# Leaving out the matmuls that TensorE runs beside the triangular solve, in an attention and expert layer on one core

## The reference, cut to what matters

```
h = silu(causal_conv4(rms(x)))
q, k, v = norm(h @ wq), norm(h @ wk), h @ wv
mem = 0.9 * mem + (h @ w_spike)_t                 # membrane
spike = mem > 0.5;  mem = mem - 0.5 * spike
alpha = sigmoid(ab_t + alpha_spike * spike);  beta = sigmoid(bb_t + sum(spike * beta_spike))
s = s * alpha
s = s - beta * k (k' s) + beta * k v'             # delta rule, s is 64 x 128 for each head
out = q' s
```

## Time and profile before

| | |
|---|---|
| median of 3 runs | 2338.61 us (2329.96 to 2342.53) |
| span of the profiled execution | 2335.2 us; its own time outside the span is not given |
| TensorE busy | 1920.2 us (82%), 18624 records |
| VectorE busy | 1336.8 us (57%) |
| ScalarE, GpSimd busy | 692.3 us (30%), 287.5 us (12%) |
| mean granted TensorE clock | 0.895 |
| the matmuls of L836 | 230.8 us busy, 480 records |

### The profile page before, as it was taken

How to read it: one execution, slowest core, us unless ns; L and a number is a source line. 1 busy time by engine, 2 the same in 40 slices (tenths; PEclk the granted TensorE clock), 3 DMA queues, 4 the chain that set the end, 5 groups by cost and what they waited for, 6 DMA issues and landing times. The chain is left out here.

```text
span 2335.2 us, 47728 instructions
## 1 busy us (share of the span) xinstructions
PE 1920.2 (82%) x18624; PEld 1181.7 (51%) x18624; DVE 1336.8 (57%) x3245; ACT 692.3 (30%) x1251; POOL 287.5 (12%) x434
## 2 busy tenths in 40 slices
PE   1378778878978877887887887787699999999998
PEld 0134544643653553463364365355366666665665
DVE  2777567558548656856765855653244444444443
ACT  1231341241232134124124223212233333333321
POOL 2210220220131131031013012101000000000000
PEclk9579979988977987997898798799689999999999
DMA  1011001001101101100200110110300000000000
GB/s 48 0 29 24 10 27 28 13 7 40 17 11 29 28 11 29 23 11 7 46 11 11 28 29 6 29 23 12 105 1 15 10 13 4 9 13 4 13 0 10
DMA packets 135620, 45.91 MB, mean 20 GB/s; under 512 B 126073, under 2 KB 126657, under 8 KB 135426
## 3 DMA queue, kind: packets, MB, share of 16 engines
q1 hardware_dynamic: 134786, 41.02, 7.2%
q0 software_dynamic: 640, 2.10, 0.3%
HBM read 26.32 MB, written 16.78 MB: 18 GB/s over the span
## 5 line engine op out<-in xcount | busy, mean ns | idle before, releaser
L836 PE MATMUL ps<-wv,ident 128*128 128x512 f32 x480 | 230.8, 630 | 37.7 <-DVEq L1189 37.6
L1653 PEld LDWEIGHTS pf<-w,hm 128*128 128x128 f32 x2048 | 237.5, 192 | 28.7 <-issue 28.7
L1653 PE MATMUL pf<-w,hm 128*128 128x128 f32 x2048 | 239.6, 275 | 0.0
L1631 PE MATMUL pf<-xh,w 128*128 128x512 f32 x512 | 233.7, 600 | 5.5 <-DVE w L1686 3.5
L443 POOL COPY kx<-kend_t 32x256 f32<-32x256 f32 x256 | 114.5, 447 | 898.0 <-PE ps L890 853.5
L1248 DVE SCALAR_TENSOR_TENSOR state<-state,gam,ps 128x128 f32<-128x128 f32 x512 | 137.6, 342 | 75.8 <-PE ps L890 75.8
L836 PEld LDWEIGHTS ps<-wv,ident 128*128 128x128 f32 x480 | 91.8, 198 | 175.1 <-issue 152.9
L1204 DVE TENSOR_TENSOR nv<-ps,nrm 128x512 f32<-128x512 f32 x64 | 44.3, 692 | 207.4 <-PE ps L778 206.8
L1631 PEld LDWEIGHTS pf<-xh,w 128*128 128x128 f32 x512 | 95.1, 192 | 125.0 <-issue 120.1
L1840 DVE TENSOR_SCALAR hm<-pf,b 128x512 f32<-128x512 f32 x128 | 96.0, 750 | 99.8 <-PE pf L1631 98.5
L1503 ACT ACTIVATE hm<-pf,b 128x512 f32<-128x512 f32 x128 | 87.0, 684 | 188.3 <-PE pf L1631 187.9
(11 more groups left out here) (231 smaller groups left out, 3346.8 us busy)
## 6 DMA issues: line engine op xcount, KB each, us to landing
b_d<-ab SPq DMA_DIRECT2D x32, 128.0 KB, 2.0
a_d<-kq_pair SPq DMA_DIRECT2D x8, 512.0 KB, 2.6
kq_blk<-a_d SPq DMA_DIRECT2D x32, 128.0 KB, 2.9
u_d<-kq SPq DMA_DIRECT2D x8, 512.0 KB, 2.6
ub<-u_d SPq DMA_DIRECT2D x128, 32.0 KB, 1.9
bb<-b_d SPq DMA_DIRECT2D x128, 32.0 KB, 2.0
w<-in_w SPq DMA_DIRECT2D x8, 512.0 KB
xt<-in_xT POOLq DMA_DIRECT2D x8, 256.0 KB, 2.9
```

Of the source, the lines that this page charges most:

```text
L836: pe.matmul(bd[k % 2].t[:, :], ident[:, :], wv[:, 0:512], start=True, stop=True)
L1631: pe.matmul(b.t[:, :], w1[:, e, P * t:P * t + P], xh[:, :], start=True, stop=True).then_inc(b.full.sem, 1)
L1653: m = pe.matmul(b.t[:, D * g:D * g + D], hm[:, e % 2, t, P * g:P * g + P], w2[:, e, t, :], start=(t == 0), stop=(t == FT - 1))
```

## The change

One number changes. The pacing loop keeps its ten waits; no matmul follows them.

```diff
-KEEP_WARM = 3
+KEEP_WARM = 0
...
             for n in range(PACES):
                 pe.wait_ge(pace.sem, pace.at(c, n + 1))
                 settle(c)
                 for k in range(KEEP_WARM):
                     pe.matmul(bd[k % 2].t[:, :], ident[:, :], wv[:, 0:512], start=True, stop=True)
```

## The result

| | before | changed |
|---|---|---|
| median of 4 runs | 2340.3 us (2329.96 to 2342.53) | 2386.95 us (2370.73 to 2391.4) |
| span of the profiled execution | 2335.2 us | 2381.1 us (2382.8 us in all) |
| mean granted TensorE clock | 0.895 | 0.832 |

The ratio is 1.019, with a 95% interval from 1.0151 to 1.0228. The forecast was slower by 15 us with a range up to 2372; the kernel became slower by 46.7 us. The sign was right, the size was three times the forecast.

A forecast was written before the change was run, and what follows sets the result against it. VectorE sets the time during the solve, TensorE's delays pass on after it. Cold starts 14.1 us, less 1.3 already in chunk 0, plus 2.4 for a missed rise: 15.2 us on 2338.6, so 2353.8 us, range 2342 to 2372.

The forecast's parts named there:

- The matmuls hide beside the solve: In the solve VectorE sets the time, so removing 230.8 us of TensorE's useless matmuls was costed at nothing.
- A shorter solve: Sign of error: the solve on VectorE should take as long as now; a shorter one would show the prediction wrong.
- The cold start: After 30 us idle, work behind the solve starts at half clock: 4.9 us cold at 0.41, 2.0 us per chunk in seven.
- the extra 2.4 us for one chunk that misses its rise: Term for one chunk in seven left cold into tile work, as in the last chunk: 4.4 us instead of 2.0.
- nothing in the change pushes the falls one way: Argument against the rival of other clock falls across chunks, which would make it faster, 2332 us; chance 0.06.
- The rival of the late clock: Tile work cannot raise the clock, so each chunk stays cold some 12 us after the solve: 33 us, 2372 us; chance 0.17.

The follow-up runs named there:

- filltile: Kernel before with useless matmuls filling the tile part's pauses (one in each of two per output projection, two ahead of tile 6's write product): 2294.7 us.
- nokeep_fill: The changed kernel (no matmul behind the ten raises) with the tile part's pauses filled by useless matmuls: 2315.3 us, ratio to the kernel before 0.99.
- last4: Kernel before with useless matmuls kept only behind the last four of the ten raises, 12 a chunk: 2352.5 us, ratio 1.0037.
- first6: Kernel before with useless matmuls kept only behind the first six of the ten raises, 18 a chunk: 2356.5 us, ratio 1.0078.
- shift24: Kernel before, all useless matmuls kept, with three more (2.4 us at full clock) ahead of the tile loop: 2372.4 us, ratio 1.0136.
- shift09: Kernel before, all useless matmuls kept, with one more (512 columns, 0.86 us) ahead of the tile loop: 2388.0 us, ratio 1.0146.
- last4_fill: Kernel before with useless matmuls only behind the last four raises and the tile part's pauses filled: 2295.9 us, ratio 0.9819.

## Why the prediction was wrong

- **The matmuls hide beside the solve:** right. `ab0` came too early to matter, and the last chunk took 6.5 us from its solve's end to its write product as before. A detail was off in the kernel's favour: VectorE's column products are 18 ns shorter on average, 111.9 against 116.3 us in all, and the solves took 4.6 us less. A shorter solve was one of my own signs of being wrong, though it is small. It does not come from TensorE's silence: the solves take 243.5 us in filltile, with all thirty matmuls, and 242.3 in nokeep_fill, with none, and the column products 117.3 and 116.3.
- **The cold start:** right, 14.2 us where the sum had 14.1 - 1.3 + 2.4 = 15.2 for it. The clock rose 5.7 us behind `ab1` on average, not 4.9, and the extra 2.4 us for one chunk that misses its rise were not needed as such: no chunk stayed cold for more than 6.9 us, so that the two errors of the sum cancel, by luck. nokeep_fill against filltile shows the same in isolation, 14.0 us in their traces.
- **The failed step:** "nothing in the change pushes the falls one way". The sum had no term for the tile and keys parts; it took them to keep the falls that they had, and a change in them stood only among the rivals, with 0.06 and in the kernel's favour. The rows gave the price: chunks of 187.0 to 194.1 us. What I left undone was to ask why the kernel before had so few falls. The tile parts of its chunks 3 to 6 take 80.2 or 80.3 us, each with one fall of 3.4 us at the same place. All five other kernels without fills had more cold tile time than its 44 us: 69 in last4, and 85 to 147 in the four whose tile parts begin later (the changed one, first6, shift24, shift09). shift24 has this without any silence in the solve, and with the pauses filled it is gone: 12 us of cold tile time in filltile and 15 in nokeep_fill, all but 2.7 of it in the last chunk. What decides at which pause the clock falls stays open. In the tile parts the rise cost 20.5 us for 48 us more of cold time, 0.42 each, about the price that the sum had used.
- **The rival of the late clock** came nearest by its number, 2372, and was wrong in its place: the clock was back at the write product, or at most 1.2 us behind it, in all seven chunks.
- The other 11.7 us, in the keys parts, came with no more cold time there than before, but it lay elsewhere. A fall of 6.8 us or more stood in the second pair of heads in six of the seven chunks before, and stands in the third pair in six of the seven now. Over the seven chunks the second and third pairs take 162.7 us in place of 158.1, and the first pair (from the end of the last tile's output projection to the end of its `kend` transposes) 88.5 in place of 80.3, with 27 and 26 us of it cold. With the pauses filled the difference vanishes (481.5 against 480.9 us), so it belongs to the timing and not to the silence; why the same cold time costs more at these places was not settled.

The Trainium skill, "TensorE: Matmul & The Clock Gate", section "Why this matters for your kernels", advises against idle gaps of over some 3 us between bursts of matmuls. By that advice the pauses of the tile part would be harmless. The traces here do not agree: pauses of 0.8 to 1.9 us inside otherwise busy stretches brought falls, and filling them is what gave 44 us.

## What to carry to other kernels

A change that moves TensorE's work in time can move the falls of its clock, and in a kernel with short pauses at fixed places that may be worth more than the work moved (here 20.5 us in the tile parts against 14.2 for the cold start); look where the clock falls in each repeat of the loop, and whether the kernel before is merely lucky there. Matmuls without use pay where TensorE sets the time behind a pause (here one in each pause of about 1 us and two in one of 1.9 us, and the last 12 of the 30 in the solve); in the keys part eight more a chunk took away half of the cold time and 7.3 us of the span. Before judging a small edit in such a kernel, fill the pauses: last4 and first6 could not be told apart without fills (2352.5 and 2356.5 us, with overlapping runs), and with fills they are 15 us apart with no overlap.

## What the runs showed of the hardware that I had not expected

- The clock stayed at half for 20.5 us in the changed kernel's tile part with TensorE busy for 18.6 of them. Behind 17.6 us of silence it rose 2.9 us after a group of 128x512 products had begun (last4_fill). The fall at the same place, 61 us behind the write product, lasted 10.2 us in chunk 0 and 20.5 in chunks 1 and 5; what decides that is open.
- A small shift is enough to lose the clock: one more matmul of 0.86 us in seven of the chunks made the tile parts cold for 147 us in place of 44 and the median 50 us longer (2388.0 against 2338.4; by the ratio's interval 13 to 55 us), and three cost 34.
- A cold microsecond cost 0.39 to 0.44 us where TensorE sets the time, and filling the keys part bought back only 0.07 to 0.09 for each.
